# The weighted sums of a softmax recurrence as one fused instruction each, and in another order

## What is computed

```python
def step(buf, q_i):                      # buf: the last 64 rows
    ki = concat([buf, zeros(B, 1, D)])   # 65 keys, the last is zero
    scores = einsum('bwd,d->bw', q_i[:, None, :] * ki, w2_w) + w2_b[0]
    alpha = softmax(scores, axis=1)
    v_i = einsum('bwd,bw->bd', ki, alpha)
    return concat([buf[:, 1:, :], v_i[:, None, :]]), v_i
```

## Time and profile before

| | us |
|---|---|
| timed runs, median of 3 | 3107.3 |
| lowest and highest | 3100.91 and 3108.63 |
| profiled execution, span from its first to its last record | 3107.4 |
| VectorE busy in it | 2382.8 |
| TensorE busy in it | 1506.1 |
| ScalarE busy in it | 1370.3 |

### The profile page before, as it was taken

The page is one execution under the profiler, slowest core; times in us unless marked ns, Lnnn a source line. Parts: engine busy times, 40 slices in busy tenths (PEclk is TensorE's granted clock), DMA queues, the critical chain, the costliest instruction groups (busy, mean ns, idle before and its releaser), DMA issues. The chain is left out here.

```text
span 3107.4 us, 48199 instructions
## 1 busy us (share of the span) xinstructions
PE 1506.1 (48%) x7936; PEld 733.5 (24%) x8061; DVE 2382.8 (77%) x15872; ACT 1370.3 (44%) x3634; POOL 173.1 (6%) x259
## 2 busy tenths in 40 slices
PE   2001010010100101001029998999889998999697
PEld 1000000000000000000012223444345442445264
DVE  6898988989889898898948886777566765676623
ACT  1233333333333333333524666556665666566532
POOL 3000000000000000000100200110002000110000
PEclk8555555555555555555558999999999999999999
DMA  4000000000000000000061111020200201010100
GB/s 105 1 1 1 1 1 1 1 1 1 1 1 1 1 1 1 1 1 1 2 138 20 52 29 25 1 63 8 43 1 1 63 17 33 1 52 18 25 1 7
DMA packets 59835, 56.63 MB, mean 18 GB/s; under 512 B 6602, under 2 KB 43124, under 8 KB 59488
## 3 DMA queue, kind: packets, MB, share of 16 engines
q1 hardware_dynamic: 59488, 53.20, 7.2%
HBM read 29.98 MB, written 22.54 MB: 17 GB/s over the span
## 5 line engine op out<-in xcount | busy, mean ns | idle before, releaser
L1026 DVE TENSOR_REDUCE nm_half<-s 128x1 f32<-128x512 f32 x1088 | 700.8, 685 | 246.7 <-PE s L1203 208.7
L197 ACT ACTIVATE ex<-row,nmax 128x65 f32<-128x65 f32 x960 | 335.9, 350 | 1005.5 <-DVE nmax L299 856.9
L951 ACT ACTIVATE pt<-s 128x512 f32<-128x512 f32 x1024 | 567.1, 596 | 415.2 <-PE s L1213 402.6
L257 DVE SCALAR_TENSOR_TENSOR junk<-ex,tab 128x65 f32<-128x65 f32 x2850 | 619.6, 218 | 3.4
L360 PE MATMUL p_s<-tab,bdg 128*128 128x32 f32 x120 | 31.9, 406 | 842.6 <-DVE tab L262 842.6
L1213 PE MATMUL s<-qs,ks 128*128 128x512 bf16 x949 | 361.8, 388 | 76.2 <-ACT pt L951 60.7
L1203 PE MATMUL s<-ks,qs 128*128 128x512 bf16 x1038 | 374.1, 390 | 28.7 <-DMA qs<-zeros 19.8
L262 DVE TENSOR_TENSOR tab<-raw,rz 128x1 f32<-128x1 f32 (+1 forms) x1890 | 286.4, 152 | 3.5
L1178 PE MATMUL p_o<-pt,va 128*9 128x512 f32 x2048 | 272.1, 604 | 3.4 <-ACT pt L951 1.3
L1239 PEld LDWEIGHTS bank<-w_W,hid 128*128 128x128 f32 x2048 | 257.8, 192 | 44.2 <-ACT hid L956 13.9
L1239 PE MATMUL bank<-w_W,hid 128*128 128x128 f32 x2048 | 262.9, 276 | 6.1 <-ACT hid L956 6.1
(11 more groups left out here) (178 smaller groups left out, 1461.9 us busy)
## 6 DMA issues: line engine op xcount, KB each, us to landing
parts_dram<-parts SPq DMA_DIRECT2D x60, 256.0 KB, 3.6
qs<-parts_dram SPq DMA_DIRECT2D x38, 192.0 KB
ks<-parts_dram SPq DMA_DIRECT2D x38, 192.0 KB
h_dram<-f SPq DMA_DIRECT2D x20, 128.0 KB, 2.6
hq<-h_dram SPq DMA_DIRECT2D x5, 512.0 KB, 5.2
x<-in_x SPq DMA_DIRECT2D x4, 512.0 KB, 8.6
w_W<-in_W SPq DMA_DIRECT2D x1, 2048.0 KB
w_W<-in_W SPq DMA_DIRECT2D x8, 256.0 KB
```

The source lines that it names most:

```text
L197: nc.scalar.activation(ex[:, r % 2, :], row[:, r % 2, 1:], ACT.Exp, bias=nmax[:, r % 2:r % 2 + 1], accum_out=z[:, r % 2:r % 2 + 1]).then_i ...
L257: nc.vector.scalar_tensor_tensor(junk[:, g, :], ex[:, k, :], 1.0, tab[:, g, r:r + ROW], ALU.mult, ALU.mult, accum_out=raw[:, g:g + 1]).the ...
L951: nc.scalar.activation(pt[:, i % 4, tokens(t)], s2[t][:, :], ACT.Exp, scale=SCALE).then_inc(s_exp, 1)
L1026: nc.vector.reduce_max(nm_half[:, t, head // 2 % 2, head % 2, q:q + 1], s1[k % 3][:, :], AX.X, negate=True).then_inc(s_max, 1)
```

## The change

The sums are made by `tensor_tensor_reduce`, which multiplies two series, scales by a scalar per partition and sums up. All four read `rz` as this scalar, and their results go straight into the table; `raw`, `normalised` and two semaphores are gone. The order in a step is: reciprocal, new row's sum, score sum, maximum, first coefficient sum, shuffle, second coefficient sum. `s_coef` now counts twice in a step, so TensorE and GpSimd wait for `2 * L * (c + 1)` where they waited for `L * (c + 1)`.

```diff
             def weighted(g, k, r, done):
-                nc.vector.scalar_tensor_tensor(junk[:, g, :], ex[:, k, :], 1.0, tab[:, g, r:r + ROW], ALU.mult,
-                                               ALU.mult, accum_out=raw[:, g:g + 1]).then_inc(done, 1)
-
-            def normalised(g0, g1, k, r, done):
-
-                nc.vector.tensor_tensor(tab[:, g0:g1, r + WIN:r + ROW], raw[:, g0:g1].unsqueeze(2),
-                                        rz[:, k:k + 1].unsqueeze(1).broadcast_to((P, g1 - g0, 1)),
-                                        ALU.mult).then_inc(done, 1)
+                nc.vector.tensor_tensor_reduce(junk[:, g, :], ex[:, k, :], tab[:, g, r:r + ROW], rz[:, k:k + 1], 0.0,
+                                               ALU.mult, ALU.add, accum_out=tab[:, g, r + WIN:r + ROW])\
+                    .then_inc(done, 1)
...
                     nc.vector.reciprocal(rz[:, k:k + 1], z[:, k:k + 1]).then_inc(s_rz, 1)
                     if not last:
-                        weighted(0, k, r, s_raw_score)
-
                         dve.wait_ge(s_row, L * c + r + 2)
-                        dve.wait_ge(s_rz, n + 1)
-                        nc.vector.scalar_tensor_tensor(junk[:, 3, :], ex[:, k, :], rz[:, k:k + 1],
-                                                       row[:, 1 - k, 0:ROW], ALU.mult, ALU.mult,
+                        dve.sem_inc(s_pace, 1)
+                    dve.wait_ge(s_rz, n + 1)
+                    if not last:
+                        nc.vector.tensor_tensor_reduce(junk[:, 3, :], ex[:, k, :], row[:, 1 - k, 0:ROW],
+                                                       rz[:, k:k + 1], 0.0, ALU.mult, ALU.add,
                                                        accum_out=row[:, 1 - k, WIN:ROW]).then_inc(s_new, 1)
-                    if r:
-                        dve.wait_ge(s_coef, n)
-                    weighted(1, k, r, s_raw)
-                    if not last:
+                        weighted(0, k, r, s_score)
                         dve.wait_ge(s_new, (L - 1) * c + r + 1)
                         nc.vector.reduce_max(nmax[:, 1 - k:2 - k], row[:, 1 - k, 1:], AX.X, negate=True)\
                             .then_inc(s_max, 1)
-                        dve.wait_ge(s_raw_score, (L - 1) * c + r + 1)
-                        normalised(0, 1, k, r, s_score)
-                    weighted(2, k, r, s_raw)
+                    if r:
+                        dve.wait_ge(s_coef, 2 * n)
+                    weighted(1, k, r, s_coef)
                     if r < L - 2:
                         dve.wait_ge(s_score, (L - 1) * c + r + 1)
                         dve.sem_inc(s_pace, 1)
                         nc.vector.stream_shuffle(row[:, k, :], tab[:, 0, r + 1:r + 2 + ROW], [r + 2] * L)\
                             .then_inc(s_row, 1)
-                    dve.wait_ge(s_raw, 2 * n + 2)
-                    normalised(1, 3, k, r, s_coef)
+                    weighted(2, k, r, s_coef)
```

More of the change, by code:

```diff
@@ L82, in window_attention @@
         junk = sb("junk", [P, 4, ROW])
-        raw = sb("raw", [P, 3])
         pf = ps("pf", [P, 2, 4 * P])
@@ L105, in window_attention @@
                                                    sem("s_new"), sem("s_coef"))
-        s_raw, s_raw_score, s_score = sem("s_raw"), sem("s_raw_score"), sem("s_score")
+        s_score = sem("s_score")
         s_clear = sem("s_clear")
@@ L170, in _ @@
                 nc.gpsimd.tensor_copy(qn[:, :], qt[:, c + 3, :]).then_inc(s_qn, 1)
-                pool.wait_ge(s_coef, L * (c + 1))
+                pool.wait_ge(s_coef, 2 * L * (c + 1))
                 pool.wait_ge(s_pv, c + 1)
@@ L357, in _ @@
                     nc.tensor.matmul(p_s[q, 0:L], qn[:, q], vt1[:, q], start=True, stop=True)
-                pe.wait_ge(s_coef, L * (c + 1))
+                pe.wait_ge(s_coef, 2 * L * (c + 1))
                 for g in range(2):
```

## The result

The changed kernel takes 3125.6 us (median of 4 runs, 3123.9 to 3126.9) against 3105.9 of the kernel before on the same chips: a ratio of 1.0068, interval 1.0054 to 1.0083. It is slower, by 20 us and not by the 74 forecast; 3125.6 is inside the wide range of the prediction and outside the forecast's own, 3155 to 3215.

What follows compares the result with a forecast made beforehand. Nearly the whole step was taken as VectorE's queue, ScalarE ending last by 0.04 us. The step grows 0.08 us, 930 times: 3107 + 74 + 4 - 5 = 3180 us; own range 3155 to 3215, wide range 3098 to 3340.

Steps and rivals of the forecast that it cites:

- The price of a fused sum: Each fused sum in a step: spacing 0.21 us, near 285 ns with the per-partition scalar, separate read-out kept.
- a free scalar: Fused sums: the scalar costs nothing, spacing 0.15, step 1.22 us, -130 us, so 2975; chance 0.13.
- a sum in one record: Fused sums: no separate read-out, spacing 0.20, gap ahead of mask load goes, step 1.32, 3070 us; chance 0.05.
- the one with a gap ahead of the score sum and of the next reciprocal: Step: gaps of 0.07 and 0.10 us there, or dearer fused sums, +0.15 to +0.25 a step, 3240 to 3340; chance 0.28.
- gap and mask load 0.13: Between first coefficient sum and shuffle: idle gap 0.10 plus mask load 0.03 us, kept in the new step.
- VectorE now ends last: Behind the maximum: VectorE's part takes 0.82 us against ScalarE's unchanged 0.72, so VectorE sets the step's end.
- reciprocal and release 0.20: Step's start: new row's sum starts 0.20 us behind the reciprocal, two waits and a pace increment fitting in.
- The last step of a chunk: Chunk's end and loop turn: last record starts at 0.62 against 0.48, +0.14 us, 30 times, +4 us.
- The holes: Single steps, six or seven a chunk, with 0.19 us extra; a seventh goes with fewer records, -5 us.
- the fourth rival: Whole kernel: no change, fused sum's spacing within 0.003 of 0.19, 3098 to 3117 us; chance 0.04.
- the first's: Whole kernel: still slower, from an unseen fused price or added gaps, 3240 to 3340 us; chance 0.28.
- the third rival: Fused sums: one record writes the sum, no read-out; ScalarE's 0.72 decides, -37 us, 3070; chance 0.05.

Runs made afterwards that it cites:

- constant scale: Changed kernel with the constant 1/64 in place of `rz` as scale of the three sums going into the table; 3072.5 us, ratio 0.9903.
- the exchange of the two instructions in the kernel before: Kernel before with first normalisation and first coefficient sum changing places around the maximum; 3058.5 us, ratio 0.9857.
- the fastest kernel: Kernel before, none fused: shuffled row's wait ahead of the reciprocal, shuffle moved up, coefficients' normalisation put off to the next step; 3032.5 us, ratio 0.9781.
- the wait ahead: Changed kernel with the wait for the shuffled row and the pace increment moved ahead of the exponential's wait and the reciprocal; 3086.2 us, ratio 0.9942.
- the order without fusion: Kernel before in the changed kernel's order, with its own unfused sums and both normalisations; 3106.1 us, ratio 1.0010.

## Why the prediction was wrong

**The price of a fused sum** was right: spacing 0.21 and 0.20, 281 to 286 ns, read-outs kept. The constant scale shows that it is the operand. The rivals with a free scalar and with a sum in one record are out, and so is the one with a gap ahead of the score sum and of the next reciprocal.

The read-outs are there in the same number, 2850 and 930 in the kernel before and in the changed one, 83 ns each in the changed one.

Fewer instructions are not by themselves faster here. In one and the same order the fused sums, with two instructions fewer in a step, cost 4.7% (3249.2 us). They paid only where a sum cost about the same, 221 ns against 218: 3072.5 us against 3106.1 in the same order, with the constant scale. And a wait with its increment does cost here: moving the two gave 39 us.

**The failed step** is the term "gap and mask load 0.13" in the sum of the new step. I took the 0.10 us ahead of the mask load as a fixed cost behind a read-out and carried it over. It was the shuffle's wait for the first normalisation, which the change removes, as the exchange of the two instructions in the kernel before shows. Gap and mask load measured 0.01 in the changed kernel, and VectorE's part behind the maximum 0.68 in place of 0.82 (the last sum's 0.20 for 0.21 is the rest of that difference).

**The second step** that failed follows from it: "VectorE now ends last". With 0.68 it does not; ScalarE's 0.73 do, as before. So of the 0.14 only 0.09 were gained, 0.82 less 0.73.

**A third term was too small**: "reciprocal and release 0.20". It measured 0.256, because of the wait and the pace increment, which I had put inside the 0.20. My row for it had no such instruction between the two. So a gap did stand where the forecast put none, ahead of the new row's sum. Moving them gives the 0.06 back. With both corrections the sum is 0.256 + 0.211 + 0.208 + 0.725 = 1.400, which is what is measured. Against the median step of the kernel before, 1.367 and not the 1.36 of the one step that I had read, that is +0.033 x 930 = +31 us and not +74.

**The last step of a chunk**, forecast at +4 us, came out at nothing. The turn of the loop, from the last reciprocal to the next chunk's first, is 5.22 us against 5.23 (medians). The last record does start later, 0.75 us behind the last reciprocal in place of 0.48, but the next chunk's copy starts 3.57 behind it in place of 3.58. It does not follow the last record, as the prediction had it; what it follows is not shown.

**The holes** were in the forecast with -5 us and gave more. The rest of the chunk went from 6.2 to 5.7 us, 30 x 0.5 = 15 us, and +31 - 15 is the +16 of the loop. They are not where the prediction had them. It has six or seven a chunk, in a place that moves. In the traces they do not move: in the kernel before, the steps 2, 9, 16, 22 and 29 of a chunk (counted from 0) are longer than the others in all 30 chunks, by 0.08 to 0.30 us, 1.0 us a chunk together. In the changed kernel it is the steps 1, 10, 17 and 25, by 0.06 to 0.22 us, and step 26 is 0.06 shorter: 0.5 us together. So one hole has gone and the others cost less. Why they cost less is argued and not shown: in a step with a late VectorE the reciprocal does not wait for ScalarE, and the next sum follows it sooner, as in this piece of the changed kernel's timeline (0.19 instead of 0.25):

```profile
700.93 0.15 DVE L279 RECIPROCAL rz<-z 128x1 f32<-128x1 f32 x1
701.12 0.28 DVE L285 CUSTOM_DVE_ANT_0 junk<-ex,row,rz 128x65 f32<-128x65 f32 x1
```

What a hole costs thus depends on where it falls. Where VectorE has time to spare it costs nearly nothing: the fused kernel in the old order has some 0.15 us of VectorE idle in each step, and its rest is (1603.5 - 58.0) / 29 - 31 x 1.549 = 5.3 us, the turn of the loop and nothing more. In the fastest kernel, with little to spare, it is (1392.2 - 57.3) / 29 - 31 x 1.267 = 6.8 us.

What makes the holes was not tried, but the trace has a trail. The page of the kernel before lists a DMA queue (packets, MB, share of 16 engines) that the profile calls "instruction":

```profile
q14 instruction: 276, 2.26, 0.2%
```

Its packets of 8 KB come seven times in every chunk of this kernel, and six times in the changed one, which has one hole less. Two of them belong to the turn of the loop; each of the others starts about 1 to 4 us behind the start of a step with a hole. TensorE and GpSimd do nothing in the steps from 12 on, so they do not make the holes there. That the packets make the holes is not shown; no run tested it.

**What was luck.** 3125.6 lies in the wide range only because that range runs from the fourth rival's 3098 to the first's 3340 across the space between them; none of the cases that it was made of gives this time. And the third rival had what came about, no gap ahead of the mask load and ScalarE last, for a reason that did not come true: it let the gap go with the read-outs, which stayed.

## What to carry to other kernels

An idle gap in front of an instruction can belong to what that instruction waits for, as the 0.10 us ahead of the mask load did, which went to 0.01 once the first normalisation ended early. So look for the end of that producer before you carry the gap into a forecast as a cost of the instruction that came ahead. In this loop, which passes between two engines, only the work between the partner's answer and the next request was paid in full; the rest was free while it was shorter than the partner's time (0.68 us against ScalarE's 0.73). So try the dear instructions behind the request and the cheap ones ahead of it: the same fused sums took 3249.2 us with three of them ahead of the maximum and 3125.6 with two. A wait with an increment on its own, behind an instruction that waits for another engine, can cost time even if it has long been met (0.06 us a step here). Put it ahead, but only if it is met well before, as in the fastest kernel, where the shuffle ends 0.22 us ahead of the reciprocal; or behind an instruction that takes longer anyway, as the wait alone stood behind the fused score sum in the old order, with the next sum 0.21 us behind that sum's start and no gap, where the kernel before had 0.13 and a gap of 0.07.

## What the runs showed of the hardware

- A scalar per partition as an operand costs 60 ns in the fused instruction (281 in the changed kernel against 221 with the constant scale) and 67 in the plain one (285 against 218), all on 128x65 tiles.
- The fused instruction writes its sum with a read-out of its own, 83 ns in the changed kernel, as the plain one does, 83 ns in the kernel before.
- A wait with an increment between a reciprocal that waits for ScalarE and the next sum costs 0.06 us (0.256 in the changed kernel against 0.199 with the wait ahead). Between a reciprocal that does not wait and the same sum it costs nothing (0.19 in the order without fusion).
- In the three kernels with the wait for the shuffled row ahead of the reciprocal and the shuffle still late, the reciprocal starts 0.15 to 0.16 us (medians; least 0.14) behind the end of the shuffle. In the fastest kernel, where that distance is 0.22, it starts 0.03 behind ScalarE's end.
- The loop has extra time in the same steps of all 30 chunks, five in the kernel before (0.08 to 0.30 us) and four in the changed one (0.06 to 0.22 us), each followed, about 1 to 4 us behind the step's start, by an 8 KB packet of the DMA queue called "instruction".
